# The residue of a whole adjacency tile made by one VectorE instruction instead of two

## The reference

```
d  = sum(adj, axis=1);      s0 = 1 / (sqrt(d) + 1e-8)
x1 = layernorm(x + s0[:,None] * (adj @ (s0[:,None] * (x @ W0 + b0))))
e  = d + 1;                 s1 = 1 / sqrt(e)
y  = s1[:,None] * ((adj + I) @ (s1[:,None] * (x1 @ W1))) + b1
out = layernorm(x1 + relu(y))
```

## Time and profile before

| what | value |
|---|---|
| median of 3 runs | 2034.13 us (2033.93 to 2034.5) |
| profiled execution, first to last instruction (span) | 2030.9 us |
| median of the runs above that span | 3.2 us |
| TensorE matmul busy | 1732.3 us, 85% |
| VectorE busy | 1606.5 us, 79% |
| ScalarE busy | 901.7 us, 44% |
| granted TensorE clock, mean | 0.939 of full |
| DMA | 574.65 MB, mean 283 GB/s |

### The profile page before, as it was taken

The page is one execution under the profiler, slowest core; times in us unless marked ns, Lnnn a source line. Parts: engine busy times, 40 slices in busy tenths (PEclk is TensorE's granted clock), DMA queues, the critical chain, the costliest instruction groups (busy, mean ns, idle before and its releaser), DMA issues.

```text
span 2030.9 us, 20449 instructions
## 1 busy us (share of the span) xinstructions
PE 1732.3 (85%) x7584; PEld 1414.4 (70%) x7584; DVE 1606.5 (79%) x2115; ACT 901.7 (44%) x1038; POOL 68.6 (3%) x131
## 2 busy tenths in 40 slices
PE   0345678899999988966999999999999989999996
PEld 0234466777787777855788888888888777777774
DVE  7999999999998889865565555554554899999996
ACT  0112334444445444533344444444434666666663
POOL 0000000000000000000000000000000000000000
PEclk9777889999999999977999999999999999999998
DMA  9988898897887756534565666565665999999991
GB/s 389 417 355 348 351 369 325 360 371 305 316 311 281 275 210 259 213 132 146 194 231 207 228 214 222 207 223 192 226 208 198 368 420 365 355 356 367 367 370 67
DMA packets 86242, 574.65 MB, mean 283 GB/s; under 512 B 10464, under 2 KB 10720, under 8 KB 20608
## 3 DMA queue, kind: packets, MB, share of 16 engines
q1 hardware_dynamic: 76320, 541.23, 68.9%
q0 software_dynamic: 9824, 32.12, 4.5%
HBM read 557.32 MB, written 15.99 MB: 282 GB/s over the span
## 4 chain that ended last, share of the span: by engine, by line
PE 61%; DVE 30%; issue 6%; DMA 2%; ACT 1%; SPq 0%; DVEq 0%; POOL 0%; ACTq 0%
PE acc L667 18%; PE acc L668 17%; PE acc L669 17%; DVE run L796 10%; DVE low L785 9%; PE part L674 3%; PE part L676 3%; DVE rowsum L805 2%; DMA lent<-adj_tiles 2%; PE mixed L618 1%; DVE o L774 1%; DVE stats L760 1%; DVE z L907 1%; PE turned L587 1%; DVE biased L827 1%
## 5 line engine op out<-in xcount | busy, mean ns | idle before, releaser
L667 PE MATMUL acc<-high,feat_high 128*128 128x512 f32 x2048 | 827.9, 404 | 177.5 <-DVE low L785 165.4
L669 PE MATMUL acc<-high,feat_low 128*128 128x512 f32 x2048 | 815.6, 398 | 0.0
L668 PE MATMUL acc<-low,feat_high 128*128 128x512 f32 x2048 | 815.6, 398 | 0.0
L785 DVE TENSOR_TENSOR low<-own,high 128x1024 fp32r<-128x1024 f32 x432 | 511.6, 1222 | 211.4 <-ACT high L691 208.5
L667 PEld LDWEIGHTS acc<-high,feat_high 128*128 128x128 f32 x2048 | 395.7, 193 | 275.4 <-issue 183.2
L691 ACT CAST high<-own 128x1024 fp32r<-128x1024 f32 x432 | 443.8, 1053 | 308.5 <-PE acc L669 253.3
L691 ACT CAST high<-lent 128x1024 fp32r<-128x1024 f32 x382 | 391.2, 1051 | 205.2 <-PE part L676 121.9
L785 DVE TENSOR_TENSOR low<-lent,high 128x1024 fp32r<-128x1024 f32 x382 | 448.9, 1222 | 25.9 <-ACT high L691 22.1
L669 PEld LDWEIGHTS acc<-high,feat_low 128*128 128x128 f32 x2048 | 394.3, 193 | 86.8
L668 PEld LDWEIGHTS acc<-low,feat_high 128*128 128x128 f32 x2048 | 395.7, 193 | 81.3
L796 DVE TENSOR_TENSOR run<-run,lent 128x2048 f32<-128x2048 f32 x99 | 226.5, 2288 | 5.4 <-DMA lent<-adj_tiles 1.9
(11 more groups left out here) (70 smaller groups left out, 577.5 us busy)
## 6 DMA issues: line engine op xcount, KB each, us to landing
lent<-adj_tiles SPq DMA_DIRECT2D x264, 1024.0 KB, 9.2
own<-adj_tiles SPq DMA_DIRECT2D x248, 1024.0 KB, 5.6
x_in<-x_rows POOLq DMA_DIRECT2D x32, 256.0 KB, 4.1
sums_rows<-stage POOLq DMA_DIRECT2D x29, 256.0 KB, 6.4
sums_in<-sums_rows POOLq DMA_DIRECT2D x29, 256.0 KB, 5.1
x_t<-x_cols SPq DMA_DIRECT2D x16, 256.0 KB, 9.4
x_rows<-x POOLq DMA_DIRECT2D x16, 256.0 KB, 3.0
out_rows<-o POOLq DMA_DIRECT2D x16, 256.0 KB, 3.9
```

The costliest lines, as they stand in the source:

```text
L667: nc.tensor.matmul(bank, f_high, a_high[:, chunk], start=(u == plan.first[g] and q == 0), stop=False)
L668: nc.tensor.matmul(bank, f_high, a_low[:, chunk], start=False, stop=False)
L669: mm = nc.tensor.matmul(bank, f_low, a_high[:, chunk], start=False, stop=(u == plan.last[g] and q == Q - 1))
L785: nc.vector.tensor_tensor(low(m), raw(n)[:, half * HALF:(half + 1) * HALF], high(m).bitcast(F32), ALU.subtract).then_inc(low_ready, 1)
```

## The change

One VectorE instruction makes the residue of the whole tile. It waits for both casts of the take. `low_ready` counts takes instead of halves, and TensorE waits for it once for each take, ahead of half 0. The casts, the half buffers, `halves_used` and the order of all steps stay. SyncE's wait for a free slot stands for the same event, counted anew.

```diff
@@ Plan
+        for u in range(self.end):
+            (ring0, b0), (ring1, b1) = self.buffer[2 * u], self.buffer[2 * u + 1]
+            assert ring0 == ring1 and b1 == b0 + 1
@@ sync
-                        sp.wait_ge(low_ready, 2 * plan.take_of[m] + 2)
+                        sp.wait_ge(low_ready, plan.take_of[m] + 1)
@@ tensor
+                pe.wait_ge(low_ready, u + 1)
                 for half in range(2):
                     a_high, a_low = high(2 * u + half), low(2 * u + half)
-                    pe.wait_ge(low_ready, 2 * u + half + 1)
@@ vector
                 if kind == "low":
                     n = takes[i][0]
-                    for half in range(2):
-                        m = 2 * i + half
-                        dve.wait_ge(high_ready, m + 1)
-                        nc.vector.tensor_tensor(low(m), raw(n)[:, half * HALF:(half + 1) * HALF],
-                                                high(m).bitcast(F32), ALU.subtract).then_inc(low_ready, 1)
+                    ring, b = plan.buffer[2 * i]
+                    dve.wait_ge(high_ready, 2 * i + 2)
+                    nc.vector.tensor_tensor(low_ring[ring][:, b:b + 2, :].rearrange("p b n -> p (b n)"), raw(n),
+                                            high_ring[ring][:, b:b + 2, :].rearrange("p b n -> p (b n)").bitcast(F32),
+                                            ALU.subtract).then_inc(low_ready, 1)
```

## The result

The changed kernel takes 2069.66 us (2068.53 to 2071.28, 4 runs) against 2034.03 us (2033.79 to 2034.5, 4 runs): ratio 1.0177, 95% interval 1.0163 to 1.0192, 35.6 us slower. The profiled execution was the slowest of the four (2071.28 us), with a span of 2069.2 us against 2030.9, so the traces differ by 38.3 us.

What follows compares the result with a forecast made beforehand. It took TensorE and VectorE to set the end by turns. Terms -6.7 + 19.3 + 3.6 + 4.3 + 6.7 = +27.2 us on 2034.1 gave 2061 us; own range 2051 to 2066, widened 2047 to 2077.

Steps and rivals of the forecast that it cites:

- rival D: Longer TensorE stalls bring a lower clock: 2076 us if in sweep 1 alone (chance 0.10), 2094 with sweep 3 (0.05).
- Fewer instructions: VectorE's queue saves 0.07 us a take on 95 takes of the chain in sweeps 1 and 3: -6.7 us.
- Half 0 late: At 18 crossings in sweeps 1 and 3 where TensorE stands waiting, half 0 is usable 1.07 us later: +19.3 us.
- Before 393 us VectorE does not fall behind: Up to 393 us, with DMA at 0.91, later residues delay no loads: nothing added.
- Second cast: VectorE also waits for half 1's cast at row starts in sweep 1 and behind `y_t` in sweep 3: +3.6 us.
- cast crossings: At four places in sweep 1 the whole residue, not half 1's, follows the cast, 1.07 us more each: +4.3 us.
- Sweep 2: TensorE 0.5 us late at 11 row starts and 0.12 at 10 takes behind ScalarE's features: +6.7 us.
- Sweep 3: From 1579 us to the end about +9 us; TensorE's waits on residues grow from 24.6 us to some 45.
- Loads: SyncE's wait for the residue ends up to 1.07 us later, but DMA has slots to spare: nothing.
- Rival A: VectorE's queue counts everywhere but sweep 2 and TensorE's late starts are absorbed: 2014 us, or 1988; chance 0.06.
- Rival B: `y_t` waits hide half of sweep 3's longer stalls and the ring's slack hides sweep 2: 2049 us; chance 0.13.
- Rival C: Gain and loss cancel if only sweep 1's crossings count and a take saves 0.16 us: 2034 us; chance 0.03.

Runs made afterwards that it cites:

- E3: The kernel before, still two residue instructions a take, but VectorE waits for both casts and TensorE for both residues: 2077.55 us, ratio 1.022.
- E1: The kernel before, with two residue instructions a take, but TensorE waits for both residues ahead of half 0: 2059.65 us, ratio 1.0131.
- E4: The change in sweep 1 alone (151 takes whole), two residues a take elsewhere as in the kernel before: 2051.51 us, ratio 1.0088.
- E12: The changed kernel, but the first 42 takes (up to 393 us) keep two residue instructions: 2067.69 us, ratio 1.0167.
- E2: The kernel before, but VectorE waits for both casts of a take ahead of its first residue, still two instructions: 2044.89 us, ratio 1.0059.
- E5: The change in sweep 2 alone (120 takes whole), two residues a take elsewhere as in the kernel before: 2042.07 us, ratio 1.0043.
- E6: The change in sweep 3 alone (136 takes whole), two residues a take elsewhere as in the kernel before: 2043.58 us, ratio 1.005.
- E7: The kernel before, with each half's matmuls that need only high run ahead of TensorE's wait for the residue: 2008.9 us, ratio 0.9881.

## Why the prediction was right, and where its sizes were off

Direction and mechanism were right: TensorE gets half 0 late, VectorE waits for a second cast, the saving is small. 2069.7 us lies in the range of 2047 to 2077; the predicted 2061 is 8.7 us under it. It lies above the forecast's own bounds, 2051 to 2066: the range reached up to it only because it was widened for rival D, the clock, and the traces give the clock at most about 1 us of the difference (below). That the result fell inside the range is in this part luck.

By stretches, in us, the sum's own terms and the two traces give this (the terms for sweep 1 make +12, not the +11 that the prediction states; the traced run is 1.6 us above the median):

| stretch of before | by the sum | by the traces |
|---|---|---|
| up to the crossing at 393 us | -1.8 | +3.4 |
| from there to 887 us | +13.8 | +16.0 |
| layer 0's last steps and sweep 2 | +6.7 | +9.8 |
| sweep 3 | +8.5 | +9.1 |

Term by term:

- **The instruction's duration** (2.29 us, from the sum of a tile): measured 2288 ns. Right.
- **Fewer instructions, -6.7 us by 0.07 us for a take**: E3 against the changed kernel gives -8 to -9 us for 407 takes, so some more takes than my 95 lie on the path, or E3's path is not the same one. With the rival price of 0.16 us the same takes would make about -15 us. That price follows from the Trainium skill, "VectorE: DVE Perf Modes", section "The DRAIN you can't avoid", as I read it; the section also says that an instruction that is not held starts earlier, and with that the trace agrees. In the changed kernel a sum starts 236.34 - 234.14 = 2.20 us after the residue's start, which has a duration of 2.28:

```profile
234.14 2.28 DVE L769 TENSOR_TENSOR low<-own,high 128x2048 fp32r<-128x2048 f32 x1
236.34 2.28 DVE L781 TENSOR_TENSOR run<-run,lent 128x2048 f32<-128x2048 f32 x1
```

- **Half 0 late, +19.3 us**: E1 alone costs 26.9, but not all of that belongs to this term. In its trace 4.7 us are in sweep 2 and 2.2 before 393 us; the rest of sweep 1 has 9.2 and sweep 3 10.5, close to what the other 17 crossings make at 1.14 us each, the length of E1's second residue. In the changed kernel TensorE is later by 1.07 us at each of the row starts at 444, 498 and 555 us of before. Number and price of the crossings were right.
- **"Before 393 us VectorE does not fall behind"**: this step failed. By the sum the stretch should have given -2.9 us, and with the crossing at its end -1.8; it was +3.4 in this trace, 2.6 in E4's, and E12, 2.0 us below the changed kernel, points the same way. The queue saving is there (folds of rows 0 to 3 come 0.2 to 0.8 us early), but I let TensorE be late for free in a stretch where its late half buffers come back to VectorE as late casts, in rows 5 and 6, for which the change makes VectorE wait.
- **Second cast +3.6 and cast crossings +4.3**: E2 alone costs 12.1 us. The same order, 4 us short. The row starts at 613, 676, 743 and 813 us were as I said (stalls of 4.86 us where there were 3.45, 1.07 + 0.34 more). But at the ends of rows 12 to 15 TensorE became 1.4 to 1.9 us later, not 1.07, and row 11 got a crossing it had not had.
- **Sweep 2, +6.7 us**: 8.7 by E5. The row start was 0.65 us and not 0.5 (the cast of 1.06, the residue of 2.29 and the gaps between them make 3.53 us), and there were nine of them, not 11; the takes behind ScalarE's features lost about 0.3, not 0.12.
- **Sweep 3, some +9 us**: 9 by the traces, 10.3 by E6. Right. But what I wrote of its waits (from 24.6 to some 45 us) was not: 32.5, because only the nine crossings lengthened and not all 21 waits.
- **Loads, nothing**: right as far as the traces show; VectorE's sums wait for landing tiles 3.8 us in both.
- **Rival A** (faster) fell: sweep 3, where VectorE is 91% busy, lost 10 us. **Rival B** (absorbed) fell too. **Rival C** as well.
- **Rival D**, the clock, is not what is missing. At the row start at 444 us of before it looks like it: the granted clock over the next 7.6 us was 0.74 and is 0.61 behind the stall that is 1.07 us longer. At 498 us it is 0.67 in both kernels, and at 555 us it is the other way round. From the first matmul after the stall, the kernel before at 444, 498 and 555 us, then the changed kernel at the same takes:

```profile
444.06:451.66 7.60, 7.59 (x25) 6.10 (x26) 7.60 (x10) 5.81 (x7) 0.00 (x0) 0.74 0.79 284
497.64:505.24 7.60, 7.60 (x23) 6.05 (x24) 7.60 (x10) 5.33 (x7) 0.00 (x0) 0.67 0.52 191
554.45:562.05 7.60, 7.60 (x21) 5.97 (x22) 7.60 (x10) 3.80 (x4) 0.00 (x0) 0.59 0.63 259
```

```profile
448.31:455.91 7.60, 7.60 (x21) 6.03 (x22) 7.58 (x7) 3.83 (x4) 0.00 (x0) 0.61 0.80 293
503.90:511.50 7.60, 7.60 (x23) 6.06 (x24) 5.40 (x6) 4.27 (x5) 0.00 (x0) 0.67 0.55 171
561.76:569.36 7.60, 7.60 (x23) 6.06 (x24) 5.31 (x6) 3.08 (x4) 0.00 (x0) 0.66 0.67 267
```

Take for take TensorE lost 0.9 us behind the first of these stalls, nothing behind the second, and won 0.5 behind the third; over the seven row starts from 444 to 813 us losses and gains add up to 0.9 us. The 1.7 us more at each of nine stalls that I priced for this rival are in no trace. Such differences also stand between executions of the same code: in the trace of E6, whose sweeps 1 and 2 are those of before, TensorE is up to 0.5 us early and up to 2.3 us late in sweep 1, though from 393 us on its stalls have the same length. So a difference of one or two us between single traces says little.

In sweep 3 the granted clock fell once in the changed kernel, behind a stall of 2.51 us, and not in the kernel before:

```profile
1733.83:1738.28 4.45, 4.45 (x13) 3.31 (x13) 4.28 (x11) 2.71 (x3) 2.05 (x4) 0.62 0.75 279
```

It cost nothing. The next take started without the wait for its residue that it had before (1.52 us at 1706.48), and TensorE was 31.8 us late there as at the take before (31.9). E5, with sweep 3 as before, had two such falls and was as late at the sweep's end as at its start, 8.9 us. The Trainium skill, "TensorE: Matmul & The Clock Gate", section on HAM oscillation, has waits between bursts bring the lower clock back each time. In sweep 1 the traces agree, at all these row starts, before and after; in sweep 3, with stalls up to 2.6 us, they mostly do not.

## What to carry to other kernels

Merging two instructions is paid by whoever waits for the first: count the places where the consumer stands still at the first part, and price each at the difference of the two durations (1.07 us), against the start-to-start saving (0.07 us) on the producer's path. Do not grant the lateness for free in a stretch where the producer is the bound; look for the place at which it waits for the consumer in turn, here through a buffer that is given back late. Ask also what the merged instruction must wait for that its first part did not (here the second cast). And where a consumer waits for the slower of two inputs, first give it all the work that needs only the other: that was worth 32 us here, nearly as much as the change cost.

## What was not expected

Running the high matmuls first gained 24.4 us in E7, where 18 crossings x 0.88 us make 16. The trace shows where a good part of the rest may lie: the clock. At the two row starts that were at 444 and 498 us TensorE's stall is 1.59 us instead of 4.59, and the granted clock stays at 1.00 behind it, where it had been 0.74 and 0.67:

```profile
440.61:448.21 7.60, 6.33 (x26) 4.88 (x27) 7.43 (x19) 6.61 (x10) 0.00 (x0) 1.00 0.81 286
491.12:498.72 7.60, 6.32 (x26) 4.87 (x27) 7.43 (x19) 6.61 (x10) 0.00 (x0) 1.00 0.71 249
```

At the other row starts of sweep 1 it falls here too. From the crossing at 393 us to the one at 887 us the mean is 0.96 against 0.94, which is 37 us at 1.2 GHz against 57; half of the difference, 10 us, is an estimate of the most that it gave, out of 16.4 us that TensorE won in this stretch. In sweep 3, up to the last take, E7's trace has 7 us at 1.2 GHz, the kernel before none. This trace is of E7's fastest run, with a mean clock of 0.943; the other three had 0.939 to 0.941. No run tested the clock alone.

How much the whole residue costs depends on the order around it: 36 us in the kernel as it was, 7 us with the high matmuls of a take first, and it gains 3 us where TensorE is far behind. It is no property of the instruction.
